# A transposed input loaded by columns instead of transposed on TensorE, in an attention and mixture-of-experts block

## The chip, the cores and the metric

The program runs on one core of a Trainium2 chip. The metric is the device time of one execution in microseconds (us); of several executions the median is given. A core has five engines with an instruction stream each: TensorE (PE, matrix products and transposes; PEld is its loading of weights), VectorE (DVE), ScalarE (ACT), GpSimd (POOL) and SyncE (SP), which here only issues transfers. Sixteen DMA engines move the data.

## The reference

The input x has 32 sequences of 256 tokens with 128 features, all in float32. Two layers follow, each with a residual and a normalisation:

```python
def attn(x):                                   # 16 heads of width 64
    q = einsum('bse,hed->bhsd', x, Wq) + bq    # k and v alike
    scores = where(causal, einsum('bhsd,bhtd->bhst', q, k) / 8, -inf)
    out = einsum('bhst,bhtd->bhsd', softmax(scores), v)
    return out.transpose(0, 2, 1, 3).reshape(32, 256, 1024) @ Wo + bo
def ffn(x):                                    # 8 experts, two for each token
    xn = norm(x) * gamma + beta
    w, idx = top_k(softmax(xn @ router_w.T / 1.5), 2)
    h = silu(einsum('btd,edf->betf', xn, W1))
    return x + sum_e(wdense[e] * (h[e] @ W2[e]))
x = norm(x + attn(x))
x = norm(ffn(x))
```

## The kernel before

The first stage is attention. It goes through the 32 sequences (n) and, within each, through four steps (q = 0 to 3); d = 4n + q counts the steps. A step treats two pairs of heads: the scores of step d, the transposes of the probabilities and the output of earlier steps, and the projections of query and key for step d + 1. Every engine has its own hand-written order of work, and semaphores join them. The second stage is the experts' work on tokens that GpSimd has sent to a queue in HBM, and the third is the sum and the last normalisation. Only attention is touched.

Queries, keys and values come from the transposed input, features on partitions and tokens in columns. It is held as two parts, xt_hi (rounded) and xt_lo (the rest), in two buffers each. SyncE loads a sequence by rows into x_raw (two buffers; 256 rows of 512 bytes). In step q == 2, TensorE transposes the two 128x128 blocks of the next sequence into the PSUM tile ps_f (transpose_input), ScalarE rounds ps_f into xt_hi, and VectorE subtracts to get xt_lo (rest_of_xt). The tile ps_f also serves the values' projection and the output projection, which is why TensorE waits for res_done before the transposes and for xt_lo_done after them. GpSimd reads x_raw a second time: it adds the bias and keeps the residual xb, in step q == 3 (residual_input), and signals xb_done.

SyncE's queue serves its transfers in the order in which they are issued. It starts with x_raw of sequence 0, six parts of the three projection weights (wqkv), x_raw of sequence 1 and Wo (wo_sb). After the constants are ready come zeroes for the queue in HBM, W1 of all experts and W2, 2 MB each. In step q == 0 of a sequence it issues the rows of the next one, once the buffer is free:

```python
if q == 0 and 1 <= n < SEQS - 1:
    sp.wait_ge(xt_ready, n)
    sp.wait_ge(xb_done, n)
    sp.dma_start(x_raw[:, (n + 1) % 2], ...)
```

In sequences 1 and 2 the kernel also splits W1 for the second stage, one expert e per step. ScalarE rounds it into w1_part (it waits for w1_loaded, and from e = 2 on for w1_stored, since w1_part has two buffers), VectorE subtracts, and SyncE stores the result to w_split in HBM:

```python
act.wait_ge(w1_loaded, 16)
if e >= 2:
    act.wait_ge(w1_stored[e % 2], e // 2 * 16)
act.activation(w1_part[:, e % 2, 0].bitcast(F32R), w1_raw[:, e], ACT.Copy)
```

Of the kernel before, what the change touches and what calls it, by code (L numbers as in the profile page):

```python
# [5 lines left out]
F32 = mybir.dt.float32  # L6
# [4 lines left out]
ALU = mybir.AluOpType  # L11
# [18 lines left out]
def postln_block(nc, x, wq, wk, wv, bq, bk, bv, wo, bo, gamma, beta, router_wt, w1, w2, out):  # L30
# [27 lines left out]
    with ExitStack() as ctx:  # L58
# [45 lines left out]

        x_raw = sb("x_raw", [P, 2, TILES, D])
        xb = sb("xb", [P, TILES, D])
        xt_hi = sb("xt_hi", [P, 2, S], F32R)
        xt_lo = sb("xt_lo", [P, 2, S], F32R)
        qk = sb("qk", [P, 2, 2, S])
# [86 lines left out]
        ps_f = psum("ps_f", [P, 512])  # L196

        x_loaded = [sem("x_loaded_even"), sem("x_loaded_odd")]
        attn_w_loaded = [sem("attn_w_loaded_%d" % i) for i in range(6)]
        small_loaded = sem("small_loaded")  # L200
        wo_loaded = sem("wo_loaded")
# [132 lines left out]
        @block.sync  # L334
        def _(sp):
            def load_x(n):
                sp.dma_start(x_raw[:, n], x[n].rearrange("(i p) d -> p i d", p=P)).then_inc(x_loaded[n], 16)

            load_x(0)
            for half in range(2):  # L340
                cols = slice(half * 512, (half + 1) * 512)
                for i, w in enumerate((wq, wk, wv)):
                    sp.dma_start(wqkv_raw[:, i, cols], w[:, cols]).then_inc(attn_w_loaded[half * 3 + i], 16)
            load_x(1)
            sp.dma_start(wo_sb[:], wo.rearrange("p (c d) -> p c d", c=PAIRS)).then_inc(wo_loaded, 16)
            sp.wait_ge(consts_ready, 1)
            sp.dma_start(queue[E * CAP:E * CAP + ROWS].rearrange("(i p) d -> p i d", p=P),
                         empty[:, 0:BLOCKS]).then_inc(spare_zeroed, 16)
            sp.dma_start(w1_raw, w1.rearrange("p (e c) -> p e c", e=E)).then_inc(w1_loaded, 16)
            sp.dma_start(m_w2[:], w2).then_inc(w2_loaded, 16)  # L350

            def step(n, q, d):
                if q == 0 and 1 <= n < SEQS - 1:
                    sp.wait_ge(xt_ready, n)
                    sp.wait_ge(xb_done, n)
                    sp.dma_start(x_raw[:, (n + 1) % 2], x[n + 1].rearrange("(i p) d -> p i d", p=P)
                                 ).then_inc(x_loaded[(n + 1) % 2], 16)
                if n in (1, 2):
                    e = d - QUADS
                    sp.wait_ge(w1_lo_done, e + 1)  # L360
                    sp.dma_start(w1_split[:, e], w1_part[:, e % 2].rearrange("p k c -> p (k c)")
                                 ).then_inc(w1_stored[e % 2], 16)
                if q == 3 and n == SEQS - 2:
                    sp.wait_ge(tail_done, 1)
                    for e in range(E):
                        tail = sp.value_load(t_tail[0:1, e:e + 1], min_val=0, max_val=E * CAP - TAIL)
                        sp.dma_start(queue[bass.ds(tail, TAIL), :].rearrange("(p i) d -> p (i d)", p=P),
                                     empty[:].rearrange("p i d -> p (i d)")).then_inc(tails_zeroed, 16)

            sequences(step)  # L370

            def load_weights(j):
                buf = j % WBUFS
                if j >= WBUFS:
                    sp.wait_ge(m_rows_ready, j - WBUFS + 1)
                expert = sp.value_load(tab_e[0:1, j:j + 1], min_val=0, max_val=E - 1)
                sp.dma_start(m_w1[:, buf], w1_split[:, bass.ds(expert, 1), :].rearrange("p e (k c) -> p (e k) c", k=2)
                             ).then_inc(m_w_loaded[buf], 16)

            def load_rows(j):  # L380
                buf = j % WBUFS
                if j >= WBUFS:
                    sp.wait_ge(m_xt_ready, j - WBUFS + 1)
                    sp.wait_ge(m_gate_done, j - WBUFS + 1)
                    sp.wait_ge(m_keep_done, j - WBUFS + 1)
                row = sp.value_load(tab_x[0:1, j:j + 1], min_val=0, max_val=E * CAP)
                sp.dma_start(m_x[:, buf], queue[bass.ds(row, ROWS), :].rearrange("(i p) d -> p i d", p=P)
                             ).then_inc(m_x_loaded[buf], 16)

            for par in range(2):  # L390
                sp.wait_ge(w1_stored[par], E // 2 * 16)
            sp.wait_ge(first_table_done, 1)
            load_weights(0)
            for par in range(2):
                sp.wait_ge(tokens_sent[par], (COUNTED + 1 - par) // 2 * TILES * TOP * 16)
            load_rows(0)
            load_weights(1)
            load_rows(1)
            for j in range(NJ):
                if j + 2 == NJ1:  # L400
                    sp.wait_ge(table_done, 1)
                    sp.wait_ge(spare_zeroed, 16)
                    for par in range(2):
                        sp.wait_ge(tokens_sent[par], SEQS // 2 * TILES * TOP * 16)
                if j + 2 < NJ:
                    load_rows(j + 2)
                    load_weights(j + 2)

            for buf in range(YBUFS):
                sp.wait_ge(m_y_sent[buf], ((NJ - 1 - buf) // YBUFS + 1) * BLOCKS * 16)  # L410

            y_parts = y_tok.rearrange("(k p f r) d -> k f p (r d)", k=TOP, p=P, f=FINS)
            out_parts = out.rearrange("s t d -> (s t) d").rearrange("(p f r) d -> f p (r d)", p=P, f=FINS)

            for f in range(FINS):
                for k in range(TOP):
                    sp.dma_start(f_y[:, f, k, :], y_parts[k, f]).then_inc(f_y_loaded[f], 16)
            for f in range(FINS):
                sp.wait_ge(f_out_done, f + 1)
                sp.dma_start(out_parts[f], f_y[:, f, 0, :]).then_inc(f_out_stored, 16)  # L420
            sp.wait_ge(f_out_stored, FINS * 16)
# [155 lines left out]
        def _(act):  # L577
# [55 lines left out]
            def step(n, q, d):  # L633
# [5 lines left out]
                if d >= 2 and q in (1, 2):  # L639
                    copy_outputs(d)  # L640
                if q == 2 and n + 1 < SEQS:
                    act.wait_ge(xt_ready, n + 2)
                    act.activation(xt_hi[:, (n + 1) % 2, :], ps_f[:, 0:S], ACT.Copy).then_inc(xt_hi_done, 1)
                if q == 2 and n == SEQS - 1:
                    evacuate_second_v(n * 4 + 4, 1)
                if d < LAST:
# [81 lines left out]
        def _(dve):  # L728
# [17 lines left out]

            def rest_of_xt(count, par):
                dve.wait_ge(xt_hi_done, count)
                dve.tensor_tensor(xt_lo[:, par, :], ps_f[:, 0:S], xt_hi[:, par, :].bitcast(F32), ALU.subtract  # L749
                                  ).then_inc(xt_lo_done, 1)  # L750

            rest_of_xt(1, 0)
# [345 lines left out]
        def _(pe):  # L1098
# [72 lines left out]
            def first_filler(n, q):  # L1171
                if q == 0 and n < SEQS:
                    if n == 0:
                        pe.wait_ge(attn_w_lo, 3)
                    else:
                        pe.wait_ge(v_done, n * 4)
                    v_projection(n % 2, 0, 0)
                if q == 1 and n == 0:
                    pe.wait_ge(v_done, 2)
                    pe.wait_ge(wo_loaded, 16)  # L1180
                    pe.wait_ge(bv_wide_done, 1)
                    product(ps_f[:, 0:D], [(bv_wide[:, c, :], wo_sb[:, c, :]) for c in range(PAIRS)]).then_inc(bo_ready, 1)
                if q == 2 and n + 1 < SEQS:
                    if n == 0:
                        pe.wait_ge(bo_done, 1)
                    else:
                        pe.wait_ge(res_done, n * TILES - 1)
                    pe.wait_ge(x_loaded[(n + 1) % 2], ((n + 1) // 2 + 1) * 16)
                    transpose_input(n + 1)
                if q == 1 and n == SEQS - 1:  # L1190
                    pe.wait_ge(v_done, n * 4 + 2)
                    v_projection(n % 2, 1, 0)
                if q == 2 and n == SEQS - 1:
                    pe.wait_ge(res_done, n * TILES - 1)
                    v_projection(n % 2, 1, 1)
                if q == 3 and n < SEQS - 1:
                    if n == 0:
                        pe.wait_ge(attn_w_lo, 6)
                        pe.wait_ge(xt_lo_done, 2)
                    else:  # L1200
                        pe.wait_ge(res_done, n * TILES)
                    v_projection(n % 2, 1, 0)

            def second_filler(n, q):
# [6 lines left out]
                    output_projection(n, 0)  # L1211
                if q == 2 and n in MID:
                    if n + 1 < SEQS:
                        pe.wait_ge(xt_lo_done, n + 2)
                    else:
                        pe.wait_ge(v_done, n * 4 + 4)
                    output_projection(n, 1)
# [223 lines left out]
```

## Time and profile before

| | |
|---|---|
| median of 3 runs | 1322.31 us (1321.48 to 1324.12) |
| the profiled execution | 1320.37 us, of which the span is 1318.2 us |
| TensorE busy | 1288.0 us, 98% of the span |
| VectorE, ScalarE, GpSimd busy | 84%, 82%, 38% |
| DMA packets | 58,860 with 98.19 MB |
| mean granted TensorE clock | 0.996 of full speed |

The span reaches from the first instruction to the last; the time of the execution is a little longer. A busy share says how much of the span an engine worked, not whether another one waited for it; the chain that ended last and the waits say that. A packet is one contiguous piece that a DMA engine moves.

### The profile page before, as it was taken

To read this page: it belongs to the slowest core of one execution; us is meant where nothing else is said; L and a number is where in the kernel's file an instruction comes from. 1 tells how busy PE (TensorE), PEld (TensorE's weight loads), DVE (VectorE), ACT (ScalarE), POOL (GpSimd) and SP (SyncE) were. 2 spreads that over 40 slices of the span, in tenths; PEclk is the share of its full clock that TensorE was granted. 3 is DMA by queue.
4 is the path that set the end of the run, shared out by engine and by line. 5 is a ranking of instruction groups with operands and counts; after the bars stand their busy time and mean duration, and the time that the engine had idled before them with its cause. 6 is when DMAs were issued, how large, how long until landed. Compare 5 with 4: busy or idle time off the path is not lost.

```text
span 1318.2 us, 36163 instructions
## 1 busy us (share of the span) xinstructions
PE 1288.0 (98%) x11298; PEld 1141.5 (87%) x11298; DVE 1102.1 (84%) x5209; ACT 1078.2 (82%) x3481; POOL 498.7 (38%) x1067
## 2 busy tenths in 40 slices
PE   7999999999999999999999999999998999999997
PEld 6888888888888888888888888888887999999983
DVE  6888888888888888888888888888886898888856
ACT  7888888888888888888888888888885777777737
POOL 1013333333333333333333333333333675665645
PEclk9999999999999999999999999999998999999999
DMA  5011000000000000000000000000033587777748
GB/s 211 35 67 46 14 14 17 15 18 16 16 14 14 14 14 13 14 14 14 14 14 14 14 18 16 19 16 14 14 140 92 158 239 233 236 226 233 222 137 329
DMA packets 58860, 98.19 MB, mean 74 GB/s; under 512 B 9376, under 2 KB 36131, under 8 KB 58416
## 3 DMA queue, kind: packets, MB, share of 16 engines
q1 hardware_dynamic: 49024, 78.67, 19.2%
q0 software_dynamic: 8640, 17.13, 3.8%
q8 instruction: 94, 1.54, 0.5%
q14 instruction: 94, 0.77, 0.2%
q10 hardware_dynamic: 1008, 0.08, 0.1%
HBM read 65.85 MB, written 30.91 MB: 73 GB/s over the span
## 4 chain that ended last, share of the span: by engine, by line
PE 86%; ACT 6%; DVE 4%; issue 1%; DMA 1%; POOL 0%; ACTq 0%; SPq 0%; POOLq 0%; DVEq 0%
PE ps_f L1102 15%; PE ps_b L1136 13%; PE ps_a L1102 13%; PE ps_s L1143 12%; PE ps_s L1124 9%; PE ps_s L1102 7%; PE ps_a L1327 4%; PE ps_b L1327 4%; PE ps_s L1127 4%; ACT probs L596 2%; PE ps_s L1398 2%; ACT probs L598 2%; PE ps_a L1299 1%; PE ps_s L1148 1%; PE ps_f L1168 1%
## 5 line engine op out<-in xcount | busy, mean ns | idle before, releaser
L596 ACT ACTIVATE probs<-probs,neg_max 128x256 f32<-128x256 f32 x512 | 255.3, 499 | 134.7 <-DVE neg_max L845 134.7
L472 POOL TENSOR_SCALAR ln_b<-mv 128x2 f32<-128x2 f32 x32 | 6.1, 190 | 633.7 <-DVE mv L908 633.7
L841 DVE CUSTOM_DVE_ANT_0 probs<-ps_s,mask 128x256 f32<-128x256 f32 x512 | 214.2, 418 | 29.4 <-PE ps_s L1127 26.9
L1143 PE MATMUL ps_s<-ident,probs 128*128 128x128 f32 x1536 | 200.6, 274 | 0.9 <-issue 0.8
L1136 PE MATMUL ps_b<-pt,f_y 128*64 128x256 f32 (+1 forms) x2048 | 196.9, 334 | 3.5 <-ACT f_y L591 1.6
L598 ACT ACTIVATE probs<-probs,neg_max 128x128 f32<-128x128 f32 x512 | 198.7, 388 | 0.0
L855 DVE TENSOR_SCALAR probs<-probs,inv_sums 128x256 f32<-128x256 f32 x512 | 181.9, 355 | 9.1
L1136 PEld LDWEIGHTS ps_b<-pt,f_y 128*64 128x64 f32 x2048 | 132.6, 137 | 54.4 <-issue 9.6
L562 POOL DMA_INDIRECT y_tok<-f_y,m_dest x142 | 145.8, 1027 | 83.7 <-DVE m_dest L1008 57.2
L1124 PE MATMUL ps_s<-qk 64*128 64x256 f32 x1024 | 170.7, 409 | 5.3 <-ACT pt L631 3.0
L1143 PEld LDWEIGHTS ps_s<-ident,probs 128*128 128x128 f32 x1536 | 173.0, 143 | 1.6 <-issue 1.5
L1102 PE MATMUL ps_a<-xt_hi,wqkv_hi 128*128 128x256 f32 x512 | 152.0, 297 | 0.0
L856 DVE TENSOR_SCALAR probs<-probs,inv_sums 128x128 f32<-128x128 f32 x512 | 149.5, 292 | 0.0
L845 DVE CUSTOM_DVE_ANT_0 probs<-ps_s,mask 128x128 f32<-128x128 f32 x512 | 146.3, 286 | 0.0
L941 DVE COPY pt<-ps_s 128x768 f32<-128x768 f32 x128 | 122.0, 953 | 28.1 <-PE ps_s L1143 27.9
L1102 PE MATMUL ps_a<-xt_hi,wqkv_lo 128*128 128x256 f32 x512 | 143.4, 280 | 0.0
L1102 PE MATMUL ps_a<-xt_lo,wqkv_hi 128*128 128x256 f32 x512 | 143.0, 279 | 0.0
L530 POOL DMA_INDIRECT queue<-z,slot_now x128 | 127.2, 994 | 39.9 <-issue 29.9
L1102 PE MATMUL ps_f<-wo_sb,f_y 128*128 128x128 f32 x1024 | 124.7, 275 | 0.0
L1102 PE MATMUL ps_s<-m_xhi,m_w 128*128 128x256 f32 x568 | 119.8, 294 | 2.3 <-DVE m_xlo L1025 1.5
L585 ACT ACTIVATE qk<-ps_a,bq_sb 128x256 f32<-128x256 f32 x256 | 118.5, 463 | 1.6 <-DVE bq_sb L756 1.6
L1102 PEld LDWEIGHTS ps_f<-wo_sb,f_y 128*128 128x128 f32 x1024 | 119.3, 192 | 0.2 <-DVE xt_lo L749 0.2
(205 smaller groups left out, 3144.4 us busy)
## 6 DMA issues: line engine op xcount, KB each, us to landing
m_w<-w_split SPq DMA_DIRECT2D x71, 512.0 KB
m_x<-queue SPq DMA_DIRECT2D x71, 133.0 KB
f_y<-y_tok SPq DMA_DIRECT2D x32, 256.0 KB, 6.6
queue<-empty SPq DMA_DIRECT2D x8, 532.0 KB, 4.8
x_raw<-in_x SPq DMA_DIRECT2D x32, 128.0 KB, 2.1
w_split<-f_y SPq DMA_DIRECT2D x8, 512.0 KB, 3.2
out_x<-f_y SPq DMA_DIRECT2D x16, 256.0 KB, 6.4
y_tok<-f_y,m_dest POOLq DMA_INDIRECT x142
```

The source lines that it names most:

```text
L530: pool.indirect_dma_start(queue, bass.IndirectOffsetOnAxis(ap=slot_now[:, par, col:col + 1], axis=0), z[:, par, i, :], None).then_inc(toke ...
L562: pool.indirect_dma_start(y_tok, bass.IndirectOffsetOnAxis(ap=m_dest[:, j % (2 * YBUFS), i:i + 1], axis=0), m_y[:, j % YBUFS, i, :], None, ...
L596: act.activation(row[:, 0:2 * P], row[:, 0:2 * P], ACT.Exp, scale=-1.0, bias=neg_max[:, pair, h, 0:1], accum_out=sums[:, d % 2, pair, h, 0:1])
L598: act.activation(row[:, 2 * P:3 * P], row[:, 2 * P:3 * P], ACT.Exp, scale=-1.0, bias=neg_max[:, pair, h, 1:2], accum_out=sums[:, d % 2, pa ...
L841: dve.tensor_tensor_reduce(out=row[:, 0:2 * P], in0=ps_s[:, pair, h, 0:2 * P], in1=mask[:].rearrange("p a b -> p (a b)"), scale=-1.0, scal ...
L845: dve.tensor_tensor_reduce(out=row[:, 2 * P:3 * P], in0=ps_s[:, pair, h, 2 * P:3 * P], in1=mask[:, 1, :], scale=-1.0, scalar=-MASKED, op0= ...
L855: dve.tensor_scalar(row[:, 0:2 * P], row[:, 0:2 * P], inv_sums[:, d % 2, pair, h, 0:1], None, ALU.mult)
L856: ins = dve.tensor_scalar(row[:, 2 * P:3 * P], row[:, 2 * P:3 * P], inv_sums[:, d % 2, pair, h, 1:2], None, ALU.mult)
L1102: ins = pe.matmul(dst, lhs, rhs, start=(i == 0), stop=(i == len(terms) - 1))
L1124: pe.matmul(ps_s[:, pair, h, 0:2 * P], qk[r, pair, 0, P:2 * P], qk[r, pair, 1, :], start=True, stop=True)
L1136: ins = pe.matmul(ps_b[r, cols], v[:, k, c * P + h * DH:c * P + (h + 1) * DH], pt[:, pair, h, src], start=(k == 0), stop=(k == 1), skip_gr ...
L1143: ins = pe.transpose(ps_s[:, pair, h, dst:dst + P], probs[:, buf, pair, h, src:src + P], ident[:])
```

## The change

Each sequence is loaded a second time, by columns: partition d gets the 256 values of feature d, single elements of 4 bytes that lie 512 bytes apart in HBM. They go into a new tile xt_raw with three buffers. SyncE issues the columns of sequences 1 and 2 right behind Wo, and those of sequence n + 2 in step q == 0 of sequence n, behind the rows of n + 1. ScalarE and VectorE read xt_raw where they read ps_f. TensorE's transposes of sequences 1 to 31 and the waits for them are gone; sequence 0 is still transposed. The row-wise loads remain, for the residual. TensorE's wait for res_done, which guards ps_f, now stands before the output projection of step q == 2, in place of the wait for xt_lo_done.

```diff
+        xt_raw = sb("xt_raw", [P, 3, S])
...
+        xt_loaded = [sem("xt_loaded_%d" % i) for i in range(3)]
...
+            def load_columns(n):
+                sp.dma_start(xt_raw[:, n % 3], x[n].rearrange("t d -> d t"),
+                             allow_slow_non_contiguous=True).then_inc(xt_loaded[n % 3], 16)
+
+            load_columns(1)
+            load_columns(2)
             sp.wait_ge(consts_ready, 1)
...
                 if q == 0 and 1 <= n < SEQS - 1:
-                    sp.wait_ge(xt_ready, n)
                     sp.wait_ge(xb_done, n)
                     sp.dma_start(x_raw[:, (n + 1) % 2], x[n + 1].rearrange("(i p) d -> p i d", p=P)
                                  ).then_inc(x_loaded[(n + 1) % 2], 16)
+                if q == 0 and 1 <= n < SEQS - 2:
+                    sp.wait_ge(xt_lo_done, n)
+                    load_columns(n + 2)
...
                 if q == 2 and n + 1 < SEQS:
-                    act.wait_ge(xt_ready, n + 2)
-                    act.activation(xt_hi[:, (n + 1) % 2, :], ps_f[:, 0:S], ACT.Copy).then_inc(xt_hi_done, 1)
+                    act.wait_ge(xt_loaded[(n + 1) % 3], ((n + 1) // 3 + (1 if (n + 1) % 3 else 0)) * 16)
+                    if n >= 1:
+                        act.wait_ge(v_ready, n * 4)
+                    act.activation(xt_hi[:, (n + 1) % 2, :], xt_raw[:, (n + 1) % 3, :], ACT.Copy).then_inc(xt_hi_done, 1)
...
             def rest_of_xt(count, par):
                 dve.wait_ge(xt_hi_done, count)
-                dve.tensor_tensor(xt_lo[:, par, :], ps_f[:, 0:S], xt_hi[:, par, :].bitcast(F32), ALU.subtract
+                columns = ps_f[:, 0:S] if count == 1 else xt_raw[:, (count - 1) % 3, :]
+                dve.tensor_tensor(xt_lo[:, par, :], columns, xt_hi[:, par, :].bitcast(F32), ALU.subtract
                                   ).then_inc(xt_lo_done, 1)
...
-                if q == 2 and n + 1 < SEQS:
-                    if n == 0:
-                        pe.wait_ge(bo_done, 1)
-                    else:
-                        pe.wait_ge(res_done, n * TILES - 1)
-                    pe.wait_ge(x_loaded[(n + 1) % 2], ((n + 1) // 2 + 1) * 16)
-                    transpose_input(n + 1)
...
                     if n == 0:
                         pe.wait_ge(attn_w_lo, 6)
-                        pe.wait_ge(xt_lo_done, 2)
+                        pe.wait_ge(bo_done, 1)
...
                 if q == 2 and n in MID:
                     if n + 1 < SEQS:
-                        pe.wait_ge(xt_lo_done, n + 2)
+                        pe.wait_ge(res_done, n * TILES - 1)
```

The order of SyncE's transfers at the start decides what waits for what. Before, from x_raw of sequence 1 on (f_y<-in_w is W1, m_w<-in_w is W2, w_split<-f_y a store of a split expert, queue<-empty the zeroes):

```order
L337 DMA x_raw<-in_x 128x2x128
L345 DMA wo_sb<-in_wo 128x1024
L347 DMA queue<-empty 128x2x133 [waits consts_ready]
L349 DMA f_y<-in_w 128x4096
L350 DMA m_w<-in_w 128x4096
L356 DMA x_raw<-in_x 128x2x128 [waits xb_done,xt_ready]
L361 DMA w_split<-f_y 128x1024 [waits w1_lo_done] x4
```

The same place with the change:

```order
L339 DMA x_raw<-in_x 128x2x128
L347 DMA wo_sb<-in_wo 128x1024
L349 DMA xt_raw<-in_x 128x256x1 x2
L355 DMA queue<-empty 128x2x133 [waits consts_ready]
L357 DMA f_y<-in_w 128x4096
L358 DMA m_w<-in_w 128x4096
L363 DMA x_raw<-in_x 128x2x128 [waits xb_done]
L349 DMA xt_raw<-in_x 128x256x1 [waits xt_lo_done]
L371 DMA w_split<-f_y 128x1024 [waits w1_lo_done] x4
```

Two column loads now stand ahead of W1 and W2, and one ahead of the first four stores of w_split; the same pair of rows recurs ahead of the next four stores.

On TensorE, step q == 2 of the first sequence, from the attention output (ps_b) over the input's transposes to the projections (ps_a) of the next step, before:

```order
L1136 MATMUL ps_b<-pt,f_y 64x256 x2
L1136 MATMUL ps_b<-pt,f_y 64x128 x2
L1168 MATMUL ps_f<-ident,x_raw 128x128 [waits x_loaded_odd,bo_done]
L1168 MATMUL ps_f<-ident,x_raw 128x128
L1102 MATMUL ps_a<-xt_hi,wqkv_hi 128x256
L1102 MATMUL ps_a<-xt_lo,wqkv_hi 128x256
```

And with the change:

```order
L1149 MATMUL ps_b<-pt,f_y 64x256 x2
L1149 MATMUL ps_b<-pt,f_y 64x128 x2
L1115 MATMUL ps_a<-xt_hi,wqkv_hi 128x256
L1115 MATMUL ps_a<-xt_lo,wqkv_hi 128x256
L1115 MATMUL ps_a<-xt_hi,wqkv_lo 128x256
```

The two transposes and their wait are gone from between the two products; nothing else there has moved.

## Rows read from the trace of the kernel before

**Rows 1.** The page: busy shares, DMA packets, and the chain that ended last

```profile
PE 1288.0 (98%) x11298; PEld 1141.5 (87%) x11298; DVE 1102.1 (84%) x5209; ACT 1078.2 (82%) x3481; POOL 498.7 (38%) x1067
...
DMA packets 58860, 98.19 MB, mean 74 GB/s; under 512 B 9376, under 2 KB 36131, under 8 KB 58416
...
PE 86%; ACT 6%; DVE 4%; issue 1%; DMA 1%; POOL 0%; ACTq 0%; SPq 0%; POOLq 0%; DVEq 0%
```

**Rows 2.** GpSimd's timeline in two sequences: start us, us, engine line op

```profile
569.64 0.97 POOL L540 TENSOR_TENSOR xb<-x_raw,bo_sb 128x128 f32<-128x128 f32 x2
...
600.68 0.98 POOL L540 TENSOR_TENSOR xb<-x_raw,bo_sb 128x128 f32<-128x128 f32 x2
```

**Rows 3.** Busy time by windows, attention from 110 to 970 us

```profile
core 0: us, PE busy (x) PEld busy (x) DVE busy (x) ACT busy (x) POOL busy (x), PEclk, DMA share, GB/s
110.00:970.00 860.00, 858.81 (x7777) 750.24 (x7776) 741.65 (x3711) 744.64 (x2573) 278.33 (x731) 1.00 0.05 15
```

**Rows 4.** Waits of SyncE's queue: us in total, times, longest us

```profile
SPq L355 <- POOL xb L540: 839.4, 28, 30.8
```

**Rows 5.** The chain in order of time: start us, us, engine tile line

```profile
582.84 1.61 PE ps_a L1102 x12
...
590.50 0.37 PE ps_f L1168 x2
590.87 1.40 PE ps_a L1102 x12
```

**Rows 6.** Tile x_raw: count, ns min/median/max, first and last start

```profile
L1168 PE MATMUL ps_f<-ident,x_raw x64: 272/327/473, 4.7 to 964.0; 128*128 128x128 f32 x64
...
L356 SPq DMA_DIRECT2D x_raw<-in_x x30: 367/368/390, 23.8 to 943.5; - x30
```

**Rows 7.** Tile xt_hi on ScalarE, the same columns

```profile
L643 ACT ACTIVATE xt_hi<-ps_f x31: 365/368/377, 28.2 to 964.8; 128x256 fp32r<-128x256 f32 x31
```

**Rows 8.** DMA queues from 6 to 7 us: packets, MB, share of 16 engines

```profile
q10 hardware_dynamic: 166, 0.01, 10.3%
```

**Rows 9.** DMA queues from 7 to 8 us

```profile
q10 hardware_dynamic: 149, 0.00, 8.4%
```

**Rows 10.** DMA queues from 571.5 to 572.7 us, one load of x_raw

```profile
q1 hardware_dynamic: 272, 0.13, 36.5%
```

**Rows 11.** SyncE's timeline from 4 to 8 us, the issues

```profile
4.67 0.95 SPq L345 DMA_DIRECT2D wo_sb<-in_wo  x1
5.66 0.46 SPq L347 DMA_DIRECT2D queue<-empty  x1
6.16 0.80 SPq L349 DMA_DIRECT2D f_y<-in_w  x1
7.00 0.71 SPq L350 DMA_DIRECT2D m_w<-in_w  x1
```

**Rows 12.** DMA issues of the run: KB each, median us to landing

```profile
x_raw<-in_x SPq DMA_DIRECT2D x32, 128.0 KB, 2.1
w_split<-f_y SPq DMA_DIRECT2D x8, 512.0 KB, 3.2
...
f_y<-in_w SPq DMA_DIRECT2D x1, 2048.0 KB, 10.6
m_w<-in_w SPq DMA_DIRECT2D x1, 2048.0 KB, 14.5
...
wo_sb<-in_wo SPq DMA_DIRECT2D x1, 512.0 KB, 7.5
```

**Rows 13.** ScalarE's timeline, rounding of W1 for experts 0, 2 and 6

```profile
46.99 0.63 ACT L668 ACTIVATE f_y<-f_y 128x512 fp32r<-128x512 f32 x1
...
63.57 0.64 ACT L668 ACTIVATE f_y<-f_y 128x512 fp32r<-128x512 f32 x1
...
97.22 0.63 ACT L668 ACTIVATE f_y<-f_y 128x512 fp32r<-128x512 f32 x1
```

**Rows 14.** SyncE's timeline, the row load before the second four stores

```profile
74.37 0.39 SPq L356 DMA_DIRECT2D x_raw<-in_x  x1
```

**Rows 15.** DMA queues from 976 to 980 us, rows of 4,256 bytes

```profile
q1 hardware_dynamic: 394, 1.54, 94.7%
```

**Rows 16.** DMA queues from 10 to 12 us

```profile
q1 hardware_dynamic: 302, 0.92, 117.3%
```

## Prediction

> **What bounds the kernel now.** The page's busy shares and its chain come first: TensorE is busy for 98% of the span, and 86% of the chain that ended last is TensorE's, so a microsecond taken from it is worth nearly a microsecond [rows 1]. The stage that changes is attention: 32 sequences, about 31.0 us each (GpSimd's addition of xb starts at 569.64 and at 600.68) [rows 2]. Next come the windows: from 110 to 970 us TensorE is busy for 858.8 of 860.0 us at full clock, while the 16 DMA engines are busy for 5% [rows 3]. The DMA engines look free, and TensorE has no gap in which it waits for the input. The last reading is how early each input arrives: SyncE waits for GpSimd before each load, 839.4 us in 28 waits, and a load then lands 2.1 us later (median) [rows 4, 12]. So the input is never late now.
>
> **What is taken away.** In step q == 2 of every sequence TensorE transposes two 128x128 blocks into ps_f. The chain prices them in place. In a step without them there are 1.61 us between the end of the attention output and the next transposes of probabilities; in a step with them, 0.37 + 1.40 = 1.77 us [rows 5]. That is 0.16 us per sequence (the 272 to 473 ns of one transpose are mostly overlap) [rows 6], and 31 x 0.16 = **5.0 us** off the bounding engine. The waits that go with them (on x_loaded, on res_done, on xt_lo_done before the output projection) show no idle time in the rows; the chain runs through them without a gap. ScalarE's copy (365 to 377 ns) [rows 7] and VectorE's subtraction of the same shape now read xt_raw in SBUF. No row has these two forms from SBUF. Neither engine is on the chain at this place [rows 5], so I put them at nothing: TensorE's work for the next step covers them. Were each a fifth slower (about 0.15 us together) and the cover gone, it would be 31 x 0.15 = 4.7 us; if they were faster, nothing would follow.
>
> **What is added.** One load of 128 x 256 single elements of 4 bytes: 32,768 packets, 2,048 for each of the 16 DMA engines and one for the semaphore. Its cost rests on the time of one such packet, and the trace has no strided one. Three rows bound it:
> - From below, the small loads of ScalarE's queue (q10): gamma and beta are 128 packets of 4 bytes each, the router weights 128 of 32 bytes. Between 6 and 7 us, 166 packets took 10.3% of 16 engine-microseconds, 9.9 ns each; between 7 and 8 us, 149 took 8.4%, 9.0 ns each [rows 8, 9]. Both are times in which the engine also served large packets, so that a latency could hide.
> - From above, the nearest load with the same source, a sequence in rows of 512 bytes: 272 packets, 36.5% of 19.2 engine-microseconds, 25.8 ns each [rows 10].
> - Between them, SyncE's own time for issuing that load, at least 367 ns for 272 packets [rows 6], 1.35 ns each; if all of it were work per packet, 32,784 packets would take 44.2 us to issue.
>
> I take 9.9 ns, because its packets have the size in question. A load is then L = 2,049 x 9.9 = **20.3 us**, two thirds of the 31.0 us of a sequence. The Trainium skill (DMA: Bandwidth & Descriptors, How a descriptor splits into AXI transactions, with Why small descriptors are slow) says that a read begins at a 256-byte boundary, moves 32 bytes a cycle at 850 MHz and adds about 3 cycles. By that a 4-byte packet costs 4 to 11 cycles by its column, 7.5 on the mean: as an estimate 8.8 ns, 10.6 ns on the engine with the highest columns, and L = 21.7 us. The rows' 9.0 to 9.9 ns agree with it.
>
> **Where the 20.3 us are covered, and where not.** In the steady part a load is issued when xb_done(n) comes, in step q == 3 of sequence n-1, and it is needed in q == 2 of sequence n+1, nearly two periods later. Anything under about a period is covered there. At the start it is not. SyncE issues two column loads right behind Wo, and ahead of the queue's zeroes, W1 and W2; later the third goes ahead of the first store of w_split. One queue serves them in turn. By the rows of now, Wo lands at 4.67 + 7.5 = 12.2 us, W1 at 16.8 (4.6 behind it), W2 at 21.5 (4.7 more) [rows 11, 12]. With L ahead of them:
> 1. Columns of sequence 1 land at 12.2 + L = 32.5; ScalarE wants them at 28.2 [rows 7]. Late by 4.3.
> 2. W1 lands at 12.2 + 2L + 4.6 = 57.4; ScalarE's first rounding of W1 is at 46.99 [rows 13], or 51.3 with that delay. Late by 10.4 in all. The second columns (52.8) are in time for their use one period after the first.
> 3. W2 (4.7), the next x_raw (17 packets of 25.8 ns on an engine, 0.4) and the third columns (L) follow. Behind these stands w_split 0, which takes 9 packets of 154 ns and lands (1.4, and 0.7 for completion, an estimate within the 3.2 us from issue to landing) at 12.2 + 3L + 4.6 + 4.7 + 0.4 + 2.1 = 24.0 + 3L = 84.9 [rows 12, 15]. ScalarE's third rounding, which reuses that buffer, stands at 63.57 now [rows 13]. It becomes **3L - 39.6 = 21.3 us** late, and this holds the two earlier delays. Behind the waiting ScalarE instruction stand the exponentials and the copies of the query and key projections, so TensorE stops with it; with 98% busy it gives none of it back.
> 4. Next in line: the fourth columns are issued behind the x_raw load that stands at 74.37 now [rows 14], at about 95.7, ahead of w_split 4. They end near 116, its store near 118, and the seventh rounding comes at 97.22 + 21.3 = 118.5. That is just met.
>
> The sum against the profiled execution (span 1318.2, its time 1320.4): 1320.4 - 5.0 + 21.3 = 1336.7. The median of the runs is 1.9 above that execution, so **1338**, a change of +1.2%. In L it is 1322.3 - 5.0 - 39.6 + 3 L = 1277.7 + 3 L.
>
> **The rivals.**
> - *The load takes longer than a sequence* (chance 0.33 for L from 31.2 to 53 us, 0.12 for more). For it: the 25.8 ns row has the same source, and with each of its packets taking that, L = 52.8; the 44.2 us of issue; and the 9.9 ns were read beside other traffic. Against it: the 4-byte rows themselves. Then the DMA engines bound attention. The 31st load ends at 12.2 + 9.3 + 8 x 1.4 + 30 x 0.44 + 31 L = 45.9 + 31 L, and from xt_hi of the last sequence (964.8) 353.4 us of the span are left [rows 7], so the median is 45.9 + 353.4 + 4.1 + 31 L = 403 + 31 L (4.1 is the median less the span). This passes the forecast's own line, 1277.7 + 3 L, at L = 31.2, 15.2 ns per packet, and gives 1371 there, 1773 at 44.2 and 2040 at 52.8. Beyond that it could go if the 16 engines, which all read the same 512-byte row at nearly the same time, held each other up; no row shows such a thing. The Trainium skill (VectorE: DVE Perf Modes, The three transpose paths) calls a plain strided copy 19 times slower than the DMA transpose, which it puts at 1309 ns for 128x128. As an estimate that is 49.7 us for our 32,768 elements, and 403 + 31 x 49.7 = 1944. Nothing in the trace shows it.
> - *Faster* (0.06). One mechanism, packets that overlap inside an engine: between 10 and 12 us the packets of q1 alone sum to 117.3% of the engines' time [rows 16]. If a 4-byte packet costs under 7.3 ns, L is under 14.9 us and 3L - 39.6 is under the 5.0 us saved; under 13.2 us no stall is left and the time is 1322.3 - 5.0 = 1317. Against it: the factor needed is 1.36, and these rows' overlap is with large packets.
> - *No change that can be told* (0.04): L close to 14.9 us. Within 0.2%, 2.6 us, is about what a measurement of this kernel can tell from nothing.
>
> The forecast case, L from 15.8 to 31.2 us, has the remaining 0.45. By 1277.7 + 3 L it spans 1325 to 1371, and that is its own range (toward its end a wait at w_split 4 comes on top). **The range** for 8 in 10 is 1320 to 2040: it leaves out 0.12 above and most of the faster cases below. Its width is the factor 2.6 between two packet rows, times 31 loads. Chances: faster 0.06, same 0.04, slower 0.90.
>
> **What would show each step.** The number of packets rises from 58,860 [rows 1] to about 1.08 million (31 x 32,784 more), and the DMA share of the attention window from 5% to about 70%. The 62 matmuls of x_raw are gone, and a later sequence's period is 30.9 us instead of 31.0. ScalarE shows idle time released by xt_raw's DMA once (4 us), by W1's (6 us) and by the store of w_split (11 us); they sum to 21 us, all before 85 us. I am wrong if ScalarE waits for xt_raw in every sequence: then the packet is over 15 ns and the period is L. I am also wrong if SyncE's issue of one such load is short while the load is long, or if the x_raw rows, now queued behind columns, hold up xb.

## The result, and the profile after

The changed kernel takes **1342.63 us** (median; 1342.06 to 1343.75), beside 1321.89 us for the kernel before. The ratio is 1.0159, with a 95% interval of 1.0137 to 1.0181: slower by 1.6%, or 20.7 us. 1338 was forecast.

The page of the changed kernel answers to [rows 1]:

```profile
PE 1288.3 (96%) x11236; PEld 1140.6 (85%) x11236; DVE 1106.4 (83%) x5209; ACT 1080.3 (81%) x3481; POOL 498.2 (37%) x1067
...
DMA packets 1075163, 102.24 MB, mean 76 GB/s; under 512 B 1025680, under 2 KB 1052435, under 8 KB 1074720
...
q1 hardware_dynamic: 1065328, 82.73, 76.4%
...
PE 84%; DMA 5%; SPq 4%; DVE 3%; ACT 2%; issue 2%; POOL 1%; ACTq 0%; POOLq 0%; DVEq 0%
```

The packets are the 1.08 million that were counted ahead. TensorE has 62 matmuls fewer and its share fell from 98% to 96%, because the span grew. In the chain, DMA and SyncE's queue now hold 9% (120 us) where they held 1%; that is how long the chain runs through transfers at the start, not what they cost. The chain between 0 and 130 us names three arrivals, of W1 and of two stores of w_split. ScalarE's timeline shows them and one more, with the idle time before each instruction and what ended it (xt_hi of sequence 1, and the roundings of W1 for experts 0, 2 and 6, as in [rows 7, 13]):

```profile
30.98 0.42 ACT L655 ACTIVATE xt_hi<-xt_raw 128x256 fp32r<-128x256 f32 x1 [2.20 <-DMA xt_raw<-in_x]
...
57.93 0.63 ACT L680 ACTIVATE f_y<-f_y 128x512 fp32r<-128x512 f32 x1 [6.39 <-DMA f_y<-in_w]
...
83.61 0.63 ACT L680 ACTIVATE f_y<-f_y 128x512 fp32r<-128x512 f32 x1 [8.81 <-DMA w_split<-f_y]
...
120.61 0.63 ACT L680 ACTIVATE f_y<-f_y 128x512 fp32r<-128x512 f32 x1 [2.25 <-DMA w_split<-f_y]
```

Against the kernel before, the four instructions are 2.8, 10.9, 20.0 and 23.4 us late. From the third to the fourth, 2.25 us of the 3.4 are a wait for a transfer; the rest falls where TensorE's clock is low. While ScalarE waits, TensorE stands still (from 80 to 88 us it has no matmul). Its granted clock is 0.50, the 1.2 GHz level, from 84 to 92 us, so also when it works again, and 1.00 from 94. The same follows the wait for W1. The windows from 60 to 66 us, before and after:

```profile
60.00:66.00 6.00, 5.63 (x55) 4.83 (x53) 4.62 (x19) 4.23 (x15) 0.41 (x3) 1.00 0.05 19
```

```profile
60.00:66.00 6.00, 5.46 (x26) 5.49 (x27) 4.66 (x23) 6.00 (x23) 0.00 (x0) 0.50 1.38 142
```

TensorE is about as busy in both, with less than half of the matmuls in the second (it is not the same piece of work). No run takes this cost apart from the waits.

Nothing later waits for a column load: in the view of the tile, ScalarE waited for one once.

```profile
L349 SPq DMA_DIRECT2D xt_raw<-in_x x31: 367/469/23137, 5.7 to 937.4; - x31
L655 ACT ACTIVATE xt_hi<-xt_raw x31: 398/405/416, 31.0 to 989.3; 128x256 fp32r<-128x256 f32 x31
...
  DMA xt_raw<-in_x: 2.2, 1
...
DMA to landing us min/median/max: 21.6/22.1/44.4
```

A load lands 22.1 us after its issue. SyncE spends 469 ns on it as a rule, and more only at the start, when the loads ahead have not drained. Its timeline there, to be read against [rows 11]:

```profile
5.69 23.83 SPq L349 DMA_DIRECT2D xt_raw<-in_x  x2
29.57 19.48 SPq L355 DMA_DIRECT2D queue<-empty  x1
49.09 0.47 SPq L357 DMA_DIRECT2D f_y<-in_w  x1
```

W1, issued at 6.16 us before, is issued at 49.09.

The steady part is read from GpSimd's addition of xb, as in [rows 2], here in the kernel before and then in the changed one, the same two sequences of each, 23 apart:

```profile
165.79 0.98 POOL L540 TENSOR_TENSOR xb<-x_raw,bo_sb 128x128 f32<-128x128 f32 x2
...
880.28 0.97 POOL L540 TENSOR_TENSOR xb<-x_raw,bo_sb 128x128 f32<-128x128 f32 x2
```

```profile
189.27 0.98 POOL L550 TENSOR_TENSOR xb<-x_raw,bo_sb 128x128 f32<-128x128 f32 x2
...
904.78 0.98 POOL L550 TENSOR_TENSOR xb<-x_raw,bo_sb 128x128 f32<-128x128 f32 x2
```

The period is 714.49 / 23 = 31.07 us before and 715.51 / 23 = 31.11 us after. So 23.5 us are lost by the first of the two sequences, 1.0 us more by the second, and from there to the end of the span the changed kernel is 3.0 us shorter. The span grew by 21.5 us. The forecast period, 30.9 us, did not come. Where TensorE's saving went is in the windows from xt_hi of sequence 5 to that of sequence 31, before and after:

```profile
156.50:964.80 808.30, 807.33 (x7308) 704.88 (x7307) 696.77 (x3488) 700.01 (x2420) 266.92 (x702) 1.00 0.05 15
```

```profile
179.90:989.30 809.40, 803.49 (x7257) 700.23 (x7256) 700.31 (x3488) 701.47 (x2420) 266.82 (x702) 1.00 0.80 19
```

TensorE works 3.84 us less over 26 sequences, 0.15 each as priced, but it stands idle for 5.91 us instead of 0.97. The waits of TensorE in that window of the changed kernel (us in total, times, longest) name the releaser; before, no row of this kind stands there:

```profile
PE ps_b L1149 <- ACT f_y L601: 5.6, 26, 0.3
```

Once per sequence, the attention output of step 0 now waits for ScalarE's copy of the values. The same place in the kernel before, ScalarE's copy and TensorE's product of one sequence, and then in the changed one:

```profile
479.42 0.60 ACT L591 ACTIVATE f_y<-ps_f 128x512 f32<-128x512 f32 x1
...
480.27 1.09 PE L1136 MATMUL ps_b<-pt,f_y 128*64 128x256 f32 x10
```

```profile
472.40 0.61 ACT L601 ACTIVATE f_y<-ps_f 128x512 f32<-128x512 f32 x1
...
473.27 1.09 PE L1149 MATMUL ps_b<-pt,f_y 128*64 128x256 f32 x10 [0.21 <-ACT f_y L601]
```

TensorE starts 0.25 us after the copy's end before and 0.26 us after it with the change. In the kernel before it is 0.25 to 0.29 us in each of the 18 sequences from 165 us on. So the copy had next to nothing to spare there, although TensorE did not wait for it. ScalarE is not busy all the time either; in these windows it waits for VectorE:

```profile
ACT probs L596 <- DVE neg_max L845: 107.5, 104, 1.8
```

```profile
ACT probs L606 <- DVE neg_max L858: 99.6, 78, 1.7
```

So ScalarE alone is not the bound: what is as long as TensorE is a path that goes to and fro between ScalarE and VectorE and ends with this copy.

### The profile page after: what moved, and what is told of

Read it like the earlier page. It is cut to its first block, busy times and chain, and to the rows that moved or that the text cites. A ratio compares the mean times of both kernels' runs of the same rounds, so it can differ in the third digit from the quotient of the medians.

```text
span 1339.7 us, 36039 instructions
## 1 busy us (share of the span) xinstructions
PE 1288.3 (96%) x11236; PEld 1140.6 (85%) x11236; DVE 1106.4 (83%) x5209; ACT 1080.3 (81%) x3481; POOL 498.2 (37%) x1067
## 3 DMA queue, kind: packets, MB, share of 16 engines
HBM read 69.91 MB, written 30.91 MB: 75 GB/s over the span
## 4 chain that ended last, share of the span: by engine, by line
PE 84%; DMA 5%; SPq 4%; DVE 3%; ACT 2%; issue 2%; POOL 1%; ACTq 0%; POOLq 0%; DVEq 0%
PE ps_f L1115 14%; PE ps_a L1115 13%; PE ps_b L1149 13%; PE ps_s L1156 12%; PE ps_s L1137 9%; PE ps_s L1115 7%; PE ps_a L1333 4%; PE ps_b L1333 4%; PE ps_s L1140 4%; DMA w_split<-f_y 3%; PE ps_s L1404 2%; SPq L349 2%; SPq L355 1%; PE ps_a L1305 1%; PE ps_s L1161 1%
## 5 line engine op out<-in xcount | busy, mean ns | idle before, releaser
L1156 PE MATMUL ps_s<-ident,probs 128*128 128x128 f32 x1536 | 203.3, 277 | 5.8 <-DVE neg_max L858 5.0
L868 DVE TENSOR_SCALAR probs<-probs,inv_sums 128x256 f32<-128x256 f32 x512 | 185.1, 361 | 9.1
## 6 DMA issues: line engine op xcount, KB each, us to landing
xt_raw<-in_x SPq DMA_DIRECT2D x31, 128.0 KB, 22.1
```

What stands on the lines that cost most here:

```text
L868: dve.tensor_scalar(row[:, 0:2 * P], row[:, 0:2 * P], inv_sums[:, d % 2, pair, h, 0:1], None, ALU.mult)
L1156: ins = pe.transpose(ps_s[:, pair, h, dst:dst + P], probs[:, buf, pair, h, src:src + P], ident[:])
```

## The experiments

**Where the saving went.** Three kernels keep the changed order of the engines and vary one thing each. The first fills xt_raw by rows:

```diff
-                sp.dma_start(xt_raw[:, n % 3], x[n].rearrange("t d -> d t"), ...
+                sp.dma_start(xt_raw[:, n % 3].rearrange("p (i d) -> p i d", i=TILES),
+                             x[n].rearrange("(i p) d -> p i d", p=P)).then_inc(xt_loaded[n % 3], 16)
```

> The changed kernel, but xt_raw is filled by rows of 512 bytes instead of single elements, so the transposition is left out of the computation and only the order of TensorE, ScalarE and VectorE is that of the changed kernel. Theory 1 (the 24 us come from slow loads at the start; in later sequences TensorE's 0.16 us are given back because ScalarE, with a copy 0.04 us longer, is as long as TensorE): 1321.9 + 31 x 0.04 = 1323 us, a period of 31.13 us. Theory 2 (the saving is real, and in the changed kernel the busy DMA engines took it back): 1321.9 - 5.0 = 1317 us, a period of 30.93 us.

It took 1319.95 us, a ratio of 0.999 (0.9977 to 1.0004), and its period is (882.08 - 166.07) / 23 = 31.13 us. The time lies between the two theories (1323 and 1317 us); the period decides for the first, 31.13 us as expected and not 30.93. Without slow loads the removal of the transposes still saves nothing per sequence, so it is not the traffic that takes the saving. The second moves the rounding to GpSimd:

```diff
 # GpSimd, ahead of its norm in the next step
+                if q == 2 and n + 1 < SEQS:
+                    pool.wait_ge(xt_loaded[(n + 1) % 3], ((n + 1) // 3 + (1 if (n + 1) % 3 else 0)) * 16)
...
+                    pool.tensor_copy(xt_hi[:, (n + 1) % 2, :], xt_raw[:, (n + 1) % 3, :]).then_inc(xt_hi_done, 1)
 # ScalarE
...
-                    act.activation(xt_hi[:, (n + 1) % 2, :], xt_raw[:, (n + 1) % 3, :], ACT.Copy).then_inc(xt_hi_done, 1)
```

> As the first kernel (rows of 512 bytes in xt_raw, transposition left out), with the rounding into xt_hi done by GpSimd instead of ScalarE. Theory 1: with 0.4 us per sequence taken from ScalarE, TensorE bounds again and its 0.16 us come back: 1321.9 - 5 = 1317 us, and TensorE's wait for the copy of the values (5.6 us in 26 sequences) is gone. Rival (the wait has nothing to do with ScalarE's load, it is a chain of single waits): 1322 to 1323 us as the first kernel.

It took 1314.66 us, a ratio of 0.9948 (0.9932 to 0.9964). GpSimd's timeline of it:

```profile
166.21 0.88 POOL L550 TENSOR_TENSOR xb<-x_raw,bo_sb 128x128 f32<-128x128 f32 x2
...
877.11 0.88 POOL L550 TENSOR_TENSOR xb<-x_raw,bo_sb 128x128 f32<-128x128 f32 x2
```

The period is 710.90 / 23 = 30.91 us, 0.16 us under that of before, the price of the two transposes. TensorE's wait for the copy of the values is gone, and VectorE's waits for ScalarE's exponentials (inv_sums<-ACT probs, in the same 23 sequences) are 39.9 us instead of the 47.0 of rows_in_place, 0.31 us less per sequence. The rounding had stood ahead of exponentials that VectorE waits for. So the path through ScalarE and VectorE had to be relieved as well as TensorE. It has little to spare here either: the copy of the values ends at 448.05 us and TensorE reads it from 448.31. A rounding left on ScalarE but placed later in its order was not tried.

**Where the 23 us came from.** The loads without the rest, added to the kernel before (sequence n + 2 in step 0 as in the change; SyncE waits for the older load of the same buffer):

```diff
+            load_columns(1)
+            load_columns(2)
             sp.wait_ge(consts_ready, 1)
...
+                if q == 0 and 1 <= n < SEQS - 2:
...
+                    load_columns(n + 2)
```

> The kernel before, with the column loads added at the places of the changed kernel; nobody reads what they bring, and the input is still transposed on TensorE. Theory 1: W1 lands at 57.9 and the first store of w_split near 83.6 as in the changed kernel, so the delay is 20 to 23 us, 1342 to 1345 us, with no wait for xt_raw. Theory 3 (the delay comes from the consumers' waits for xt_raw): under 1325 us.

It took 1342.67 us, a ratio of 1.0159 (1.0141 to 1.0178), the same as the whole change. ScalarE's waits for transfers in the first 150 us:

```profile
ACT f_y L680 <- DMA w_split<-f_y: 10.9, 2, 8.8
ACT f_y L680 <- DMA f_y<-in_w: 9.9, 1, 9.9
```

The third rounding stands at 83.43 us, as in the changed kernel at 83.61. The delay needs nobody who reads the columns; it is W1 and the stores behind them in the queue. Then the opposite, the change without its loads at the start:

```diff
-            load_columns(1)
-            load_columns(2)
...
-                if q == 0 and 1 <= n < SEQS - 2:
+                if q == 0 and 3 <= n < SEQS - 2:
                     sp.wait_ge(xt_lo_done, n)
                     load_columns(n + 2)
 # and sequences 1 to 4 transposed on TensorE, with their waits, as before
```

> Sequences 0 to 4 are transposed on TensorE, and the column loads begin with sequence 5, issued in sequence 3, when W1 is split and stored. Theory 1: no wait for a transfer is left, 27 sequences at 0.04 us more than before: 1323 us. Rival (each column load costs time wherever it lies, 20 us / 31 = 0.67 us for one): 1340 us.

It took 1318.84 us, a ratio of 0.998 (0.9967 to 0.9993): 27 loads of 32,768 elements each cost nothing that can be seen. Its period, (881.93 - 166.11) / 23 = 31.12 us, is near the 31.11 us expected. The time is 4 us under the expectation; the next section compares it at equal granted clock.

**Do the three waits add up, or does the last arrival decide?** W1 and W2 ahead of the second load:

```diff
             load_columns(1)
-            load_columns(2)
...
             sp.dma_start(m_w2[:], w2).then_inc(w2_loaded, 16)
+            load_columns(2)
```

> The changed kernel with the second column load moved behind W1 and W2 on SyncE's queue. W1 should then land near 12.2 + 20 + 4.6 = 37 us, before ScalarE's 47 us, so its wait of 6.4 us is gone. Theory 1 (the last of the three arrivals decides; the first store of w_split still has three column loads, W1 and W2 ahead of it and lands near 83.6 us): 1342 us as the changed kernel, with a longer wait for the store in place of that for W1. Rival (the waits add up, each is worth itself): 1342.6 - 6.4 = 1336 us.

This run and the next two were on a chip on which the kernel before itself takes 1419.9 us, so only ratios and the first 100 us compare. The instructions also stand about 1 us later there by themselves: in from_5_gpsimd, a kernel of the last part of this section that waits for no transfer, the roundings for experts 0 and 2 start at 48.00 and 64.58 us on this chip. The ratio is 1.0145 (1.0127 to 1.0164), 20.7 us on that chip. ScalarE's roundings for experts 0 and 2:

```profile
50.87 0.63 ACT L680 ACTIVATE f_y<-f_y 128x512 fp32r<-128x512 f32 x1
...
83.93 0.63 ACT L680 ACTIVATE f_y<-f_y 128x512 fp32r<-128x512 f32 x1 [16.33 <-DMA w_split<-f_y]
```

The wait for W1 is gone and the wait for the store has grown from 8.8 to 16.3 us; the third rounding is where it was. The last arrival decides. Next, the loads of sequences 3 and 4 behind the stores as well:

```diff
 # on top of weights_first; the load now stands behind the step's store
-                if q == 0 and 1 <= n < SEQS - 2:
+                if q == (3 if n < 3 else 0) and 1 <= n < SEQS - 2:
                     sp.wait_ge(xt_lo_done, n)
                     load_columns(n + 2)
```

> As weights_first, and in sequences 1 and 2 the column load is issued in step 3, behind the stores of w_split, instead of step 0. Theory 1 by the same arrivals: 2.8 us for the first columns; the third columns are issued at 77 and land at 99, wanted at 96 (3 us); the fourth are issued at 113 and land at 135.5, wanted at 131 (4 us). In all 10 us, 1332 us. Rival (a load costs its share wherever it stands): 1342 us.

The ratio is 1.0097 (1.0076 to 1.0117), 14.1 us instead of the 10 expected. In the first 170 us ScalarE waits neither for W1 nor for a store, only for columns:

```profile
ACT xt_hi L655 <- DMA xt_raw<-in_x: 10.8, 3, 6.0
```

These 10.8 us are the expected 10. For the 3 to 4 us beyond them the same trace has a likely cause: TensorE's granted clock is 0.83, 0.66 and 0.68 in the windows 30 to 40, 100 to 110 and 140 to 150 us, around the three waits, where from_5_gpsimd on the same chip has 1.00 in each. It was not isolated. A smaller load tests the term 3 L:

```diff
-                sp.dma_start(xt_raw[:, n % 3], x[n].rearrange("t d -> d t"), ...
+                sp.dma_start(xt_raw[:, n % 3, 0:192], x[n, 0:192].rearrange("t d -> d t"), ...
+                sp.dma_start(xt_raw[:, n % 3, 192:256], x[n, 0:128, 0:64]).then_inc(xt_loaded[n % 3], 16)
...
 # ScalarE waits for twice the count of xt_loaded
```

> The changed kernel with 192 of the 256 tokens loaded by single elements and the last 64 columns of xt_raw filled by 128 rows of 256 bytes (wrong data in them, so that part of the transposition is left out). A load has 24,576 single elements, L is about 15.0 us instead of 19.9. Theory 1: the third rounding is late by 3 x 15.0 + 24 - 63.6 = 5.4 us (20.0 in the changed kernel), no other wait follows, 1321.8 + 5.4 + 1 = 1328 us. Rival (delay in proportion to the elements): three quarters of 21 us, 1337 us.

The ratio is 1.0042 (1.0026 to 1.0059), 5.4 us (1425.26 beside 1419.9). The two waits of its ScalarE:

```profile
49.97 0.63 ACT L681 ACTIVATE f_y<-f_y 128x512 fp32r<-128x512 f32 x1 [1.37 <-DMA f_y<-in_w]
...
72.23 0.63 ACT L681 ACTIVATE f_y<-f_y 128x512 fp32r<-128x512 f32 x1 [5.51 <-DMA w_split<-f_y]
```

The third rounding moved from 83.6 to 72.2 us, by 11.4; with a quarter less load, 3 x 5 = 15 was expected. Counted from the 64.58 us of from_5_gpsimd on the same chip the delay is 7.7 us, where 5.4 was expected. A quarter of the tokens gone takes 3.8 us from each of three loads instead of 5; why is open. The total is as forecast and far from three quarters of 21 us, but it is 2.3 us less than the delay, so the agreement of the total is in part luck. What the steady part adds or takes on this chip is unknown, since the kernel before left no trace there.

**The knee.** Every load twice:

```diff
...
+                sp.dma_start(xt_spare[:, n % 3], x[n].rearrange("t d -> d t"),
+                             allow_slow_non_contiguous=True).then_inc(spare_loaded[n % 3], 16)
                 sp.dma_start(xt_raw[:, n % 3], x[n].rearrange("t d -> d t"), ...
```

> The changed kernel with every column load issued twice, the first time into a tile that nobody reads. At the rate of the changed kernel, 8.6 to 8.8 ns per packet with the packets overlapped, a pair takes 36 to 40 us, more than a sequence of 31.1 us. Theory 1 (a load is free until it takes longer than a sequence): the DMA engines bound attention, ScalarE waits for xt_raw in every sequence, the period is 36 to 40 us and the time 1342 + 28 x 5 to 1342 + 28 x 9, plus 20 us at the start: 1500 to 1610 us. Rival (the engines have room for packets of a second load beside those of the first, since their shares sum to 140%): under 1400 us.

It took 1657.88 us, a ratio of 1.2532 (1.2487 to 1.2578), more than the 1500 to 1610 of the expectation. ScalarE's wait over the whole span, and DMA to landing:

```profile
  DMA xt_raw<-in_x: 213.0, 27
...
DMA to landing us min/median/max: 40.7/41.8/51.2
```

From xb at 302.82 to xb at 1276.06 there are 24 sequences of 40.55 us: the DMA engines bound it. Less 0.44 us for the row-wise load, one column load takes 20.1 us of them, 9.8 ns per packet. That is an upper bound: by slices of 1 us, the share of the DMA engines dips to 0.2, 0.1 and 0.6 from 597 to 600 us and to 0.3, 0.3 and 0.7 from 617 to 620, between the loads. The line of the first rival, 403 + 31 x 40.1, gives 1646. The expectation had missed it with the rate taken from the middle of a load, where no engine has run out of packets yet.

**A version that beats both.** columns_from_5 with the rounding on GpSimd from sequence 5 on:

> columns_from_5 with the rounding into xt_hi from sequence 5 on done by GpSimd. Theory 1: no wait for transfers, and a period of 30.91 us as in rows_gpsimd instead of 31.07: 1321.8 - 27 x 0.16 = 1317.5 us. Rival (the busy DMA engines slow GpSimd or the copies, the period stays at 31.1): 1321 to 1323 us.

The ratio was 0.9942 (0.9927 to 0.9956), on the chip of 1419.9 us. A repetition:

> The same kernel as from_5_gpsimd, on another chip, since the kernel before took 1420 us on the chip of that run and 1322 us on the others. Theory 1: a period of 30.91 us, 1321.8 - 27 x 0.16 = 1317.5 us, a ratio of 0.997. Rival (the columns' packets slow the steady part here though not in rows_gpsimd): a period of 31.1 us and a ratio of 1.000. If the ratio is 0.994 as in the first run, more than the period must have changed.

Again a chip of this kind (before: 1421.87 us), with a ratio of 0.9937 (0.9914 to 0.996), and no trace of the kernel before on it. The last two runs are a pair on one chip, the kernel before and from_5_gpsimd:

> The kernel before itself, for a trace on the same chip as the next run. Theory 1: on a chip where it takes 1322 us its period is 31.07 us and no wait is for a remote event; on a chip where it takes 1420 us both engines of the copies wait about 2 us per sequence for such an event (36 us and 24 us between 300 and 900 us in the last run), and the period is 32.3 us.

> from_5_gpsimd beside a trace of the kernel before. Theory 1: its period is 0.16 us under that of the kernel before, whatever the chip, and the time 4 us under it, a ratio of 0.997. Rival: the period is 0.3 us or more under it on a chip of 1420 us (a ratio of 0.994), because ScalarE's copy matters more there.

On this chip, one of 1322 us, the kernel before repeats itself (1321.52 us, ratio 1.0, 0.9983 to 1.0017), with a period of 31.09 us and no wait for a remote event. The other takes **1313.52 us**, a ratio of 0.9938 (0.9923 to 0.9952). GpSimd's timeline of the latter:

```profile
167.77 0.88 POOL L550 TENSOR_TENSOR xb<-x_raw,bo_sb 128x128 f32<-128x128 f32 x2
...
877.92 0.88 POOL L550 TENSOR_TENSOR xb<-x_raw,bo_sb 128x128 f32<-128x128 f32 x2
```

Its period is 30.88 us, 0.22 under that of before beside it: 27 x 0.22 = 5.9 of the 8.9 us. At equal granted clock the gap is smaller than 8.9: with a mean clock of 0.998, the two executions of this kernel took 1311.94 and 1313.66 us and the five of the kernel before beside them 1318.98 to 1319.55, 6.6 us more on the mean. The ratio is the same on both kinds of chip, so the rival (that ScalarE's copy matters more on the kind of 1420 us) has lost its reason; it is not refuted, since the period of the kernel before was not traced on such a chip.

## Why the prediction was right, and where not

- **Direction, size and place** held (the sum as written, 1336.7 + 1.9, gives 1338.6 rather than 1338): the forecast case (loads hidden in the steady part, exposed at the start) is what the trace shows, and loads_alone and columns_from_5 show it from both sides.
- **The time of one load** was the right choice between bounds that lay a factor of 2.6 apart. 20.3 us were forecast from packets of 9.9 ns; a load takes at most 20.1 us in loads_doubled, 9.8 ns per packet. That the two agree so closely is in part luck. The 9.9 ns of [rows 8] were taken "because its packets have the size in question", but the 166 packets in the trace are 155 of 4 bytes at 8.9 ns, two of 32 bytes and nine of 512 bytes at 27 ns. With 9.0 ns L would have been 18.4 us, the delay 15.7 and the forecast 1333. And a time per packet from shares is not the time that a packet adds, since packets overlap: by shares those of the changed kernel took 10.4 and 12.0 ns (last section). SyncE's 367 ns, from which 44.2 us were bounded, turned out to be a time per instruction: it spends 469 ns on 32,784 packets. My sentence that a short issue beside a long load would prove me wrong was badly aimed; it is what happened, and it changed nothing, since the DMA engines serve the queue in order whoever has been let go.
- **The arrivals**, forecast and measured: columns 32.5 and 31.0; W1 57.4 and 57.9; the store of w_split 84.9 and 83.6; delay at the third rounding 21.3 and 20.0. The seventh rounding was "just met" and in fact waited 2.25 us. The sum has no term for TensorE's clock: between the third and the seventh rounding 1.1 us more are lost without a wait for a transfer, where the granted clock is 0.50 after TensorE stood still. That makes 20.0 + 1.1 + 2.25 = 23.4 of the 23.5 us.
- **The 5.0 us saved** did not come. The step that failed is "Neither engine is on the chain at this place, so I put them at nothing: TensorE's work for the next step covers them". The chain follows the engine that ended last, and with TensorE 98% busy it ran almost through TensorE alone in this part; the path through ScalarE and VectorE did not appear in it, though it was as long. The timelines of the kernel before show it: the copy of the values ends at 480.02 us, and the product that reads it starts at 480.27, as close behind it as in the changed kernel, where TensorE waits. The 0.16 us of TensorE's work moved into that wait, and rows_gpsimd gave them back. Whether the copy from SBUF, 405 ns at the median where it was 368 [rows 7], adds the 0.04 us of the period is only argued: two traces of the kernel before differ by 0.02 us themselves.
- **The sum**: forecast -5.0 + 21.3 = 16.3. The spans give +23.5 at the start, +1.0 in the steady part and -3.0 behind it, 21.5; the medians 20.7. From the last xb to the end of the span there are 309.8 and 311.1 us in the two traces of before and 306.8 in the changed kernel, but also 304.1 (rows_in_place), 304.9 (columns_from_5) and 307.8 (loads_alone), where the code of those stages is the same. A part goes with the granted clock, which differs between executions of one kernel. From the last xb on its mean is 0.98 in the two traces of before and 0.99 or 1.00 in the four others. Beside the experiments on chips of this kind, the kernel before took 1316.73 to 1319.53 us in three executions with a mean clock of 0.999 and 1323.50 to 1326.08 in six with 0.993, while columns_from_5 took 1316.98 to 1318.32 in four with 0.999. So the 4 us that columns_from_5 lies under its expectation are no gain at equal clock, and the -3.0 is within what one kernel's executions differ by. Why the clock differs is open.
- **The rivals.** The long load (0.45 in all) has its mechanism and, within 12 us, its line confirmed by loads_doubled; the real L lay at two thirds of the threshold. Packets do overlap inside an engine, as the faster rival had it, but not by the factor that it needed.

## What to carry to other kernels

A transfer that is hidden in the steady part can still cost most where its queue also carries what the start is waiting for: list every transfer behind it in the queue, compute each arrival and take the latest delay, not the sum of the waits. A path to and fro between two other engines can be as long as the busiest engine although the chain names only that one; before pricing work taken from it, look in the timelines how long before its use each of its inputs is ready, and plan to relieve both. Add to each wait what the low clock behind it costs. Here the slow load pays only from the sequence at which the start's traffic is over, and together with a copy moved to the idle GpSimd.

## What the runs showed of the hardware

- **Single elements of 4 bytes.** Within a load the packets of an engine overlap: the shares sum to more than 100%. The queue's row between 30 and 45 us of the changed kernel, and between 573 and 583 us:

```profile
q1 hardware_dynamic: 27211, 0.11, 117.5%
...
q1 hardware_dynamic: 18680, 0.07, 139.8%
```

  By the shares a packet "took" 10.4 and 12.0 ns; by the count there were 8.8 and 8.6 ns of an engine's time for each (15 x 16 / 27,211 and 10 x 16 / 18,680). The estimate from the Trainium skill (DMA: Bandwidth & Descriptors, How a descriptor splits into AXI transactions), 8.8 ns on the mean, agrees with the latter. Its 10.6 ns for the engine with the highest columns would make a load 21.7 us, and the measured 20.1, an upper bound, lie between that and the 18.0 us of the mean. The prediction's 49.7 us came from the Trainium skill's 19 times the DMA transpose (VectorE: DVE Perf Modes, The three transpose paths). The page says it of a copy whose innermost stride in the destination is large, and gives the 1309 ns for bf16. Here that stride is one element and the type float32, so the 20.1 us do not test it.
- **The cost is a busy queue, not a busy issuer.** SyncE is held up only when the load ahead has not drained: 19.48 us for one 133 KB transfer behind two column loads.
- **The clock behind a wait.** After stretches without a matmul TensorE's granted clock is at the 1.2 GHz level for some microseconds: 0.50 from 36 to 38, from 60 to 66 and from 88 to 92 us in the changed kernel, where the kernel before has 1.00 in the same windows.
- **Two kinds of chip.** The kernel before takes 1322 us on some and 1420 us on others. In the traces of the latter kind VectorE and ScalarE wait once per sequence for an event that the profile calls remote, 36.1 and 24.4 us between 300 and 900 us (from_5_gpsimd_again), which no trace of the other kind shows. What it is stays open.
